# Softmax attention on one core: row maxima written into the stacked keys by two transfers instead of eight, and the negation taken ahead of an addition

## What is computed

```python
q, k, v = jnp.split(x @ W_attn + b_attn, 3, axis=2)   # 16 heads of 8 channels
q = _rope(q); k = _rope(k)                            # angles by head index
att = einsum('bhqd,bhkd->bhqk', q, k) / sqrt(8)
att = where(causal, att, -inf)
att = softmax(att, axis=-1)
y = einsum('bhqk,bhkd->bhqd', att, v)
return y @ W_proj + b_proj
```

## Time and profile before

| quantity | value |
|---|---|
| time before, median of 3 runs | 1124.28 us (1123.87 to 1127.2) |
| time of the profiled execution | 1126.77 us |
| its span, first to last instruction | 1125.1 us |
| mean granted TensorE clock | 0.897 |
| PE / DVE / ACT / POOL busy | 85% / 60% / 55% / 31% |
| softmax attention in the trace | about 796 to 1004 us |
| PE busy in that stretch | 147.3 us of 208 |
| transfers `stk<-mT` | 64, of 4 KB each |

### The profile page before, as it was taken

How to read it: one execution, slowest core, us unless ns; L and a number is a source line. 1 busy time by engine, 2 the same in 40 slices (tenths; PEclk the granted TensorE clock), 3 DMA queues, 4 the chain that set the end, 5 groups by cost and what they waited for, 6 DMA issues and landing times.

```text
span 1125.1 us, 12923 instructions
## 1 busy us (share of the span) xinstructions
PE 958.5 (85%) x4499; PEld 652.1 (58%) x4499; DVE 675.2 (60%) x1285; ACT 616.1 (55%) x993; POOL 347.7 (31%) x257
## 2 busy tenths in 40 slices
PE   6899998589999999789999994999566877784998
PEld 4678885133333333377888882887334544462897
DVE  2878886567787777457888836232644554316232
ACT  5455555368888888735555544534533535335443
POOL 1597776100000000006777725301011111215300
PEclk8999999789999999979999976999867788685899
DMA  5125210000000000015221201100000000001001
GB/s 164 40 76 159 66 57 19 1 0 0 1 1 0 0 1 0 1 52 120 66 66 59 55 1 56 38 1 0 1 3 3 2 2 3 2 1 38 1 1 38
DMA packets 30934, 33.63 MB, mean 30 GB/s; under 512 B 2255, under 2 KB 19991, under 8 KB 30871
## 3 DMA queue, kind: packets, MB, share of 16 engines
q1 hardware_dynamic: 30870, 32.82, 10.0%
HBM read 31.36 MB, written 1.18 MB: 29 GB/s over the span
## 4 chain that ended last, share of the span: by engine, by line
PE 65%; DVE 17%; ACT 9%; issue 3%; POOL 2%; SPq 2%; DMA 1%; ACTq 0%; DVEq 0%; POOLq 0%
PE ps L126 11%; PE ps L127 10%; PE ps L128 10%; PE ps L670 5%; PE ps L807 5%; PE ps L828 3%; PE ps L664 2%; PE ps L779 2%; PE ps L889 2%; SPq L485 2%; PE ps L648 2%; ACT L1259 2%; POOL fl L1981 2%; ACT ex L1386 1%; PE ps L898 1%
## 5 line engine op out<-in xcount | busy, mean ns | idle before, releaser
L1981 POOL TENSOR_TENSOR fl<-fp,fh 128x512 fp32r<-128x512 f32 x144 | 223.8, 1571 | 126.7 <-ACT fh L1171 126.5
L1162 ACT ACTIVATE fs<-ps 128x512 f32<-128x512 f32 x144 | 86.3, 600 | 116.6 <-PE ps L128 116.6
L1556 DVE TENSOR_TENSOR fp<-fp,cwb 128x512 f32<-128x512 f32 x128 | 140.3, 1096 | 14.0 <-DVE fp L1549 0.9
L1549 DVE TENSOR_TENSOR fp<-fs,ps 128x512 f32<-128x512 f32 x144 | 98.2, 682 | 38.8 <-ACT fs L1162 38.3
L126 PE MATMUL ps<-z_hi,w_hi 128*128 128x512 f32 x288 | 116.6, 405 | 3.3 <-DVE fp L1549 3.3
L127 PE MATMUL ps<-z_lo,w_hi 128*128 128x512 f32 x288 | 116.1, 403 | 0.0
L128 PE MATMUL ps<-z_hi,w_lo 128*128 128x512 f32 x288 | 115.4, 401 | 0.0
L1171 ACT CAST fh<-fp 128x512 fp32r<-128x512 f32 x144 | 88.8, 617 | 36.0 <-DVE fp L1556 31.8
L2046 POOL TENSOR_TENSOR ln_sq<-ln_rs 128x512 f32<-128x512 f32 x20 | 21.2, 1058 | 271.0 <-ACT ln_rs L1222 271.0
L1874 DVE TENSOR_REDUCE smax<-ps 128x8 f32<-128x2048 f32 (+1 forms) x24 | 55.0, 2291 | 53.0 <-PE ps L903 42.6
L2039 POOL TENSOR_SCALAR_AFFINE_SELECT ex<-ex 128x1024 f32<-128x1024 f32 (+1 forms) x24 | 33.7, 1406 | 169.9 <-ACT ex L1386 169.9
(11 more groups left out here) (262 smaller groups left out, 2042.7 us busy)
## 6 DMA issues: line engine op xcount, KB each, us to landing
cwb<-cw_spread SPq DMA_DIRECT2D x64, 256.0 KB, 3.2
w_raw<-in_L_ffn_w_dram SPq DMA_DIRECT2D x20, 256.0 KB, 2.9
w_raw<-in_L_ffn_w_dram SPq DMA_DIRECT2D x4, 512.0 KB, 5.6
w<-in_L_ffn_w_dram SPq DMA_DIRECT2D x8, 256.0 KB, 4.5
x_tok<-in_L_attn_x_dram SPq DMA_DIRECT2D x4, 256.0 KB, 3.7
wb<-in_L_attn_W_dram SPq DMA_DIRECT2D x1, 1024.0 KB, 7.0
wb<-in_L_attn_W_dram SPq DMA_DIRECT2D x4, 256.0 KB, 3.9
stk<-mT SPq DMA_DIRECT2D x64, 4.0 KB
```

The lines of the kernel that those rows point to most:

```text
L1162: act.activation(fs[:, n % 2, :], ps[:, n % 2, :], ACT.Silu).then_inc(silu_done, 1)
L1549: dve.tensor_tensor(f, fs[:, n % 2, :], ps[:, 2 + n % 2, :], ALU.mult).then_inc(prod_done, 1)
L1556: dve.tensor_tensor(f, f, cwb[:, x % CW_RING, :], ALU.mult).then_inc(weighed, 1)
L1981: pool.tensor_tensor(fl[:, n % RING0, :], fp[:, n % RING0, :], f32(fh[:, n % RING0, :]), ALU.subtract).then_inc(flo_done, 1)
```

## The change

Three edits, all in `attn1`.

1. On SP the eight transfers of a sequence become two, one for the high and one for the low part. Each reads 16 partitions of `mT` and writes four partitions of `stk` that are 32 apart, 16 KB in one transfer. PE waits for 32 counts of `m_placed` for each sequence in place of 128.
2. On DVE, in even steps, `maxima` (the negation) goes between the stacking of k = 2 and that of k = 3, where both came ahead of it. On PE the transposes of the maxima wait for stacking up to k = 2, and the wait for k = 3 stands behind them, ahead of `flip`.
3. On DVE, in odd steps, `maxima` goes ahead of `add`, which came first.

```diff
-                    for g in range(4):
-                        r, m = 32 * g + ROW_MAX + h, h * HEADS + g * HG
-                        sp.dma_start(f32(stk[s // SPB % 2][r:r + 1, 0, :, w]), f32(mT[m:m + HG, w])).then_inc(m_placed, 16)
+                    r, m = ROW_MAX + h, h * HEADS
+                    sp.dma_start(f32(stk[s // SPB % 2][r:r + 97:32, 0, :, w]), f32(mT[m:m + HEADS, w])).then_inc(m_placed, 16)
@@ PE, attn1
-                        pe.wait_ge(m_placed, (s + 1) * (16 * 2 * HG))
+                        pe.wait_ge(m_placed, (s + 1) * (16 * 2))
@@
                     if first and more:
-                        pe.wait_ge(stk_done, (tb + 1) * 2 * HG + 4)
+                        pe.wait_ge(stk_done, (tb + 1) * 2 * HG + 3)
                     if s + 1 < SEQS:
                         maxima(s + 1)
                     if second and tb >= 1:
                         pe.wait_ge(ln_in, u0 + NTB + tb)
+                    if first and more:
+                        pe.wait_ge(stk_done, (tb + 1) * 2 * HG + 4)
@@ DVE, attn1
                     if second and more:
                         values(tb + 1)
+                    if first and more:
+                        stack(tb + 1, range(2, 3))
+                    if s + 1 < SEQS:
+                        maxima(s + 1)
                     if second and tb >= 1:
                         add(tb - 1)
                     if first and more:
-                        stack(tb + 1, range(2, 4))
-                    if s + 1 < SEQS:
-                        maxima(s + 1)
+                        stack(tb + 1, range(3, 4))
                     if s >= 1:
                         normalise(s - 1)
```

## The result

The changed kernel took 1107.12 us, the median of four executions (1102.49 to 1107.34), against 1124.23 us for the kernel before beside it. The ratio is 0.9832 with a 95% interval of 0.9802 to 0.9863, which on 1124.28 us is 1105.4 us. It is faster, by 17 us in the medians and by 19 us by the ratio; the forecast was 14.0 us and 1110.3 us. Medians and spreads here take in all executions, while the ratios come from the fast ones alone, which leaves out two: one of `e12` and one of `four`, over 1.5% above the fastest of their kernel. The profiled execution took 1107.33 us, with a span of 1105.6 us, 19.5 us less than the one before.

A forecast was written before the change was run, and what follows sets the result against it. PE is 85% busy overall, but a chain round the engines was taken to bound the softmax attention. Gains of 10.73 + 1.32 + 1.98 = 14.0 us against the median 1124.28 gave 1110.3 us, range 1106 to 1117.

The forecast's parts named there:

- Where the chain is, and which five places count: Softmax attention: a chain round the engines; PE waits for transfers at sequences 0, 2, 4, 6 and 7, 19.1 us.
- The price of the new transfer: SP's transfers in attention: issue 0.57 us, landing 1.70; two take 2.40 us for sequence 0 in place of 6.09.
- ACT is late next at sequences 2, 4 and 6, POOL at 7: Attention: ACT's exponentials limit gains to 2.35, 2.33 and 2.21 us; POOL's masking of sequence 6 leaves sequence 7 0.15.
- The moves: DVE's negation in attention: ahead of the addition in steps 3, 5, 1.32 us; between stackings in steps 0, 2, 4, 1.98.
- the one on TensorE's clock: Attention: the granted clock falls to half in waits as before; otherwise up to 5 us gained, or as much lost.
- the rival in which the clock stays up: Attention: clock stays up at most even places, a gain of 15.5 to 19 us, 1105 to 1109; chance 0.16.
- a different number of us at half clock: Clock windows: one of three signs that would show the prediction wrong; no size given.
- the sum of 14.0: Attention: transfers 10.73 us, negation ahead of addition 1.32, negation between stackings 1.98, together 14.0 us.
- the even places right behind the waits: Attention: six projection matmuls in each of three places; without the clock's fall, 1.2 us each, with nearby products up to 5.
- The scatter of the rest: Whole execution: range 1106 to 1117 us took in the transfer's bounds and most of the clock, leaving about 0.2 out.

The follow-up runs named there:

- e12: Changed kernel with the addition left ahead of the negation in steps 3 and 5 (two transfers, negation between stackings 2 and 3): 1110.1 us, ratio 0.9853 to the kernel before.
- four: Changed kernel with four transfers for a sequence in place of two, each to two partitions of the stacked keys: 1112.7 us, ratio 0.9863 to the kernel before.
- c_after: Changed kernel run a second time, unchanged, beside the kernel before: 1106.9 us, ratio 0.9832.
- after: Changed kernel's first run, with all three edits, against the kernel before: 1107.12 us, ratio 0.9832.
- after2: Changed kernel run a third time, unchanged, beside the kernel before: 1107.5 us, ratio 0.9856.

## Why the prediction was right in its mechanism and wrong on TensorE's clock

**Where the chain is, and which five places count: right.** The waits went from 19.1 us in five places to 3.0 in one.

**The price of the new transfer: right.** Issue 0.52 us against 0.57 taken, landing 1.84 against 1.70 with 0.1 allowed for four pieces on one engine; the pair 2.50 us from first issue to landing, against 2.40, and the first exponential 3.58 us earlier against 3.69. The trace agrees with the Trainium skill ("DMA: Bandwidth & Descriptors", on why a DMA increments its semaphore by 16) on four engines after as before: eight small packets for two transfers. The about 2.0 us of the same page (Anatomy of one DMA) are for another path; on this one the landing took 1.84 us.

**ACT is late next at sequences 2, 4 and 6, POOL at 7: right**, by the rows of ACT and by the kernel with four transfers.

**The moves: right in kind; their size is not settled.** At like clock they gave 2.1 us against 3.3, by one pair of profiles. Of the 1.2 us missing, 0.65 are the later transposes behind the spare matmuls; the cause of the rest is not known.

**The step that failed** is the one on TensorE's clock: "I take it that the clock does as before." It was entered at zero, though the same paragraph had up to 5 us for it on either side, and the rival in which the clock stays up was given 0.16. It came out on that side, and so did a recorded sign of being wrong, a different number of us at half clock: 93 us between the marks in the mean before, 75 after. Between the marks the mean gain is 15.3 us, and 12.0 remain when the clock is made alike. The difference, about 3 us, is what the clock gave; it is the least certain figure here, since the changed kernel's three profiles lie 5 us apart, with windows of 0.75, 0.81 and 0.77 against 0.76, 0.74 and 0.74, and since 0.65 us of it come from the spare matmuls. Against the sum of 14.0 the attention is 1.3 us over: what the clock gave covered 2.0 us by which transfers and moves fell short, and went beyond.

Another count says the same: of the 18 us less at half clock some 12 are in the four distances with the transfers, as much as these became shorter, and the other 5 or 6, halved, are under 3 us. That is an estimate, and most of those 5 or 6 come from `c_after` alone.

The clock came back at another place than the one that I named, the even places right behind the waits. In the odd distances twelve matmuls in a row project the next block, and this happened at half clock in one execution of the changed kernel and at full clock in another. The windows between copies 5 and 6, first `after` and then `after2`:

```profile
912.60:918.10 5.50, 5.44 (x16) 3.75 (x12) 1.99 (x3) 4.12 (x5) 2.01 (x1) 0.50 0.00 0
```

```profile
919.50:922.50 3.00, 3.00 (x16) 2.13 (x12) 0.35 (x1) 2.93 (x3) 1.20 (x2) 1.00 0.00 0
```

The distance was 25.3 us in the first and 23.0 in the second, and the three odd distances together ran from 64.5 to 71.7 us against 71.7 to 72.3.

**The scatter of the rest** was not in the range either. I took the three executions shown, 1123.9 to 1127.2, for the spread of this kernel; 63 later ones beside these runs reach from 1114.7 to 1132.1. Of the 17.3 us between 1124.2 and 1106.9, some 12 are the mechanism, some 3 the clock inside the attention, and the last 2 are found outside it, in code that is the same in both. That code moves by more than this by itself: 813.6 to 819.3 us ahead of the attention and 121.7 to 126.2 us behind it in the three profiles of the kernel before. That the gain exceeds the 14.0 us is not one lucky execution, for the medians of the changed kernel were 1107.1, 1106.9 and 1107.5 us in three separate groups of runs. Whether the last 2 us are an effect of the change, through when the attention ends, or of too few profiles, stays open.

## What to carry to other kernels

When many small transfers stand in a chain, count issues times issue time first. Here seven of the eight issues were 4.4 of 6.1 us, and an access pattern that covers four destinations in one transfer took most of it away. Then ask at each place what comes next when the transfer is early; ACT or POOL capped the gain at four of five places, and a transfer one us slower would have cost nothing at three of them. In a stretch like this, where PE is busy 70% of the time, a shorter wait can also change when the clock is granted. A sum of waits should carry a term for that, and not at zero. A comparison of single profiles should begin with the same mark in code that nobody changed.

## What the runs showed of the hardware

Adding matmuls without use made the kernel before 0.5% faster (0.9948, 0.9918 to 0.9977): between the marks PE's busy time rose from 128.8 to 138.6 us and the stretch became 6.3 us shorter than in the first profile of before, with the granted clock at 0.88 in place of 0.76. Against the mean of three profiles it is 7.7 us.

Identical programs reached the attention at 813.6 to 819.3 us and spread over 17 us in total time on the chips used here. A stretch at 1.2 GHz need not stand at the same point of the program in two executions. The 24 small matmuls shown above, in code that is the same in both kernels, ran once at one level and once at the other, and so did the twelve projections in two executions of one kernel.

A transfer from 16 partitions to four cost SP 0.52 us, one from eight partitions to two 0.50 us, and one from four partitions to one 0.57 us. The first landed only 0.14 us later than the last, with four times the bytes.
